# Attention on one Trainium2 core: normalization and output of four blocks inside the group loop, in place of 14 batches at the end

## The chip, the cores and the metric

The kernel runs on one core of a Trainium2 chip. A core has TensorE (PE), VectorE (DVE), ScalarE (ACT), GpSimd (POOL) and SyncE (SP, which here only issues DMAs). They run beside one another and are ordered by semaphores. The metric is device time in microseconds (us), the median of several executions.

## The reference

A graph of 12500 nodes with 128 numbers each and 212500 edges, sorted by destination. A first layer (relation-wise products, a sum over the edges, a feed-forward part) gives `x`; the second layer is attention over each node's incoming edges:

```python
h = relu(layernorm(x))
xt = (h @ W.T + bias).reshape(n, 4, 32)
alpha = leaky_relu(alpha_src[row] + alpha_dst[col], 0.2)
ex = exp(alpha - segment_max(alpha, col)[col])
denom = segment_sum(ex, col)
alpha = ex / (denom[col] + 1e-16)
x = x + segment_sum(xt[row] * alpha[..., None], col).reshape(n, 128)
```

The kernel divides at the end: it sums `ex * xt[row]` and `ex` per node and head, and the last step is `x + sum / (denom + 1e-16)`.

## The kernel before

The nodes are 98 blocks of 128 rows (`BLOCKS`); a block lies across the 128 partitions. The edges are 104 groups of 2048 (16 chunks of 128, `CHUNKS`), sorted by destination, so a group touches one or two neighbouring blocks. `MAIN` = 103 groups go through the main loops; the last one and any that touch more blocks go through a loop over a list.

The span has three stages. To about 260 us the products of all blocks are stored as a table. To about 2440 us POOL gathers rows of that table for every group (L486, 16 indirect DMAs for a group), PE sums them per node, and after every four groups the dense part of four blocks (a quad) is computed and stored (`x_mid`, `xt_table`). The first `AHEAD` = 24 quads run in that loop; what is left, the last quad and those that touch a listed group, is in the list `redo` with its length `redo_count`, last quad first. `first_of(n)` is the first block of quad n: 0, then 4n - 2.

From about 2450 us on the attention stage runs, over 103 groups in order. POOL gathers the group's rows of `xt_table` into one of four slots of `G`, 16 indirect DMAs each; it waits for the indices and for the messages of the group four before. DVE has one round for a group: `nodes` (L1164 to L1177: maxima and state of the block), `scores` of the next group (L1152, which waits for that group's gather), `edges` (L1187 to L1194), `merge` of the group before (L1215, L1218: it adds PE's sums into `S`, which holds for each node and head 32 sums and the denominator), the selection matrix (L1198), the messages (L1204), and `prepare` for the group after next (L1135 to L1142). PE forms maxima, slots and sums from these, ACT the exponentials. The loop (L1290) has 25 iterations of four rounds; groups 101 and 102 follow written out, then the last merge (L1306).

Each DVE operation whose result the next one needs is followed by a wait on a counting semaphore (`Chain.step`). Where an index is a register, it is computed or loaded on the engine's own sequencer (`load_block`, `load_redo_count`).

The end is at L1308 to L1318: for each of 14 batches of seven blocks DVE adds 1e-16 to the denominators, takes the reciprocal, multiplies, and adds `x_res`, the layer's input, which four DMAs (L431) brought back at about 2448 us. SP stores a batch as soon as `fin_done` says so (L434 to L440). `A`, `Y` and `X` are tiles of one quad that the dense part uses and the attention stage does not.

Of the kernel before, what the change touches and what calls it, by code (L numbers as in the profile page):

```python
# [13 lines left out]
P = 128  # L14
N, E, D, R, H = 12500, 212500, 128, 8, 512
HEADS, HC = 4, 32
BLOCKS = -(-N // P)
TAIL_ROWS = N - (BLOCKS - 1) * P
CHUNKS = 16
GROUP = CHUNKS * P  # L20
GROUPS = -(-E // GROUP)
BATCH = 7
BATCHES = BLOCKS // BATCH
SPARE = BATCH
WIDE = 14
ROUNDS = BLOCKS // WIDE
TURNS = 3
FIRST_TURN = 2
XT = D + HEADS
HD = HC + 1  # L30
RUNS = 4
MAIN = GROUPS - 1
SLOTS = 4
QUAD = 4
SHIFT = 2
QUADS = -(-(BLOCKS + SHIFT) // QUAD)
LAG = 2
AHEAD = GROUPS // SLOTS - LAG
# [8 lines left out]
assert (BLOCKS + SHIFT) % QUAD == 0 and BLOCKS % WIDE == 0 and FIRST_TURN + -(-2 * CHUNKS // TURNS) <= WIDE and BLOCKS % BATCH == 0 and GROUPS % SLOTS == 0 and BLOCKS % 2 == 0 and (MAIN - 3) % SLOTS == 0  # L47
# [8 lines left out]
def first_of(n):  # L56

    return max(n * QUAD - SHIFT, 0) if isinstance(n, int) else n * QUAD - SHIFT
# [87 lines left out]
def build(nc, x, src, dst, typ, W_rel, W_self, b_conv, g1, b1n, g2, b2n, W1, b1, W2, b2,  # L146
# [7 lines left out]
    with ctx:  # L154
# [52 lines left out]
        redo = sb("redo", [1, QUADS], i32)  # L207
# [25 lines left out]
        place = sb("place", [P, 3])  # L233
        rel0 = sb("rel0", [P, CHUNKS])
# [53 lines left out]
        out_sb = g_flat[:, 0:4 * BATCH * D].rearrange("p (s b d) -> p s b d", s=4, d=D)  # L288
        inv = g_flat[:, 4 * BATCH * D:4 * BATCH * D + 4 * BATCH * HEADS].rearrange("p (s b h) -> p s b h", s=4, h=HEADS)

# [71 lines left out]

        def load_redo_count(eng):

            return eng.value_load(redo_count[0:1, 0:1], min_val=1, max_val=QUADS)
# [13 lines left out]
        def _(sp):  # L379
# [54 lines left out]
            for q in range(BATCHES):  # L434
                sp.wait_ge(fin_done, q + 1)
                lo = q * BATCH
                nb = BATCH - 1 if q == BATCHES - 1 else BATCH
                sp.dma_start(out[lo * P:(lo + nb) * P, :].rearrange("(b p) d -> p b d", p=P), x_res[:, lo:lo + nb, :]).then_inc(s_out, 16)
            sp.dma_start(out[(BLOCKS - 1) * P:N, :], x_res[0:TAIL_ROWS, BLOCKS - 1, :]).then_inc(s_out, 16)
            sp.wait_ge(s_out, 16 * (BATCHES + 1))  # L440
# [298 lines left out]
        def _(dve):  # L739
# [195 lines left out]
            c.beside(v.tensor_copy(redo[:, :], banks[2][0:1, 256:256 + QUADS]))  # L935
# [342 lines left out]
            def round_of(c, gr, s, k, first, last, landed):  # L1278

                nodes(groups, c, gr, gr, first)  # L1280
                if landed:
                    scores(groups, c, (s + 1) % SLOTS, 1 - k, landed)
                edges(groups, c, gr, s, k, (lambda: merge(groups, c, gr - 1, gr - 1, last, 1 - k)) if last is not None else (lambda: None))
# [6 lines left out]
            with dve.Fori(0, (MAIN - 3) // SLOTS) as i:  # L1290
                last = load_block(dve, i * SLOTS)
                for s in range(SLOTS):
                    gr = i * SLOTS + s + 1
                    c = Chain(dve, c_att, gr * PASS + START - MISSED)
                    first = load_block(dve, gr)
                    round_of(c, gr, (s + 1) % SLOTS, (s + 1) % 2, first, last,
                             (gathered[1][(s + 2) % SLOTS], i * (16 * CHUNKS) + 16 * CHUNKS * (1 + (s + 2) // SLOTS)))
                    prepare(groups, c, row_of(nkey_all, gr + 2), row_of(run_all, gr + 2), (s + 1) % 2)
                    assert c.n == PASS
                    last = first  # L1300
            for gr in (MAIN - 2, MAIN - 1):
                c = Chain(dve, c_att, gr * PASS + START - MISSED - (STEPS["prep"] if gr == MAIN - 1 else 0))
                last, first = load_block(dve, gr - 1), load_block(dve, gr)
                round_of(c, gr, gr % SLOTS, gr % 2, first, last,
                         (gathered[1][(gr + 1) % SLOTS], 16 * CHUNKS * ((gr + 1) // SLOTS + 1)) if gr + 1 < MAIN else None)
            merge(groups, c, MAIN - 1, MAIN - 1, first, (MAIN - 1) % 2)  # L1306

            dve.wait_ge(s_back, 16 * -(-BLOCKS // (2 * WIDE)))  # L1308
            c = Chain(dve, c_fin)
            for q in range(BATCHES):  # L1310
                s = q % 4
                lo = q * BATCH
                f = S[:, lo:lo + BATCH, :].rearrange("p b (h k) -> p b h k", h=HEADS)
                c.step(v.tensor_scalar(inv[:, s, :, :], f[:, :, :, HC:HD].rearrange("p b h o -> p b (h o)"), 1e-16, None, ALU.add))
                c.step(v.reciprocal(inv[:, s, :, :], inv[:, s, :, :]))
                c.step(v.tensor_tensor(out_sb[:, s, :, :].rearrange("p b (h k) -> p b h k", h=HEADS), f[:, :, :, 0:HC],  # L1316
                                       inv[:, s, :, :].rearrange("p b (h o) -> p b h o", o=1).to_broadcast([P, BATCH, HEADS, HC]), ALU.mult))
                v.tensor_tensor(x_res[:, lo:lo + BATCH, :], x_res[:, lo:lo + BATCH, :], out_sb[:, s, :, :], ALU.add).then_inc(fin_done, 1)  # L1318
# [246 lines left out]
```

## Time and profile before

| | us |
|---|---|
| median of 3 runs | 4616.43 (4613.22 to 4616.86) |
| the profiled execution | 4617.47 |
| its span | 4615.6 |

| engine | busy us | share of the span |
|---|---|---|
| PE (matmul) | 2439.7 | 53% |
| DVE | 2518.3 | 55% |
| ACT | 537.3 | 12% |
| POOL | 3200.9 | 69% |

The span is what the profiler records from the first to the last instruction; it stands beside the execution's own time. A share is an average over stages that have different limits, so the stage has to be looked at in which the change works. POOL's instructions here are the gathers; an idle time put down to "issue" is one in which the engine waited for nothing that the profile shows.

### The profile page before, as it was taken

To read this page: it belongs to the slowest core of one execution; us is meant where nothing else is said; L and a number is where in the kernel's file an instruction comes from. 1 tells how busy PE (TensorE), PEld (TensorE's weight loads), DVE (VectorE), ACT (ScalarE), POOL (GpSimd) and SP (SyncE) were. 2 spreads that over 40 slices of the span, in tenths; PEclk is the share of its full clock that TensorE was granted. 3 is DMA by queue.
4 is the path that set the end of the run, shared out by engine and by line. 5 is a ranking of instruction groups with operands and counts; after the bars stand their busy time and mean duration, and the time that the engine had idled before them with its cause. 6 is when DMAs were issued, how large, how long until landed. Compare 5 with 4: busy or idle time off the path is not lost.

```text
span 4615.6 us, 52499 instructions
## 1 busy us (share of the span) xinstructions
PE 2439.7 (53%) x13699; PEld 2082.5 (45%) x13804; DVE 2518.3 (55%) x6796; ACT 537.3 (12%) x1405; POOL 3200.9 (69%) x3372
## 2 busy tenths in 40 slices
PE   5952344343444444343433666666666666666664
PEld 2532333333333333333323555555555555555553
DVE  5761333333333333333333777777777777777777
ACT  2410111111111111111111000000000000000000
POOL 1057777777777777777755777777777777777772
PEclk9976666676666666666666777777787777777776
DMA  6632222222222222222213222222222222222222
GB/s 205 254 108 53 57 57 62 57 62 57 59 59 58 61 57 62 57 62 57 59 42 98 55 54 55 55 55 54 55 54 54 54 54 55 54 55 54 55 55 76
DMA packets 169505, 312.22 MB, mean 68 GB/s; under 512 B 58788, under 2 KB 99148, under 8 KB 168655
## 3 DMA queue, kind: packets, MB, share of 16 engines
q0 software_dynamic: 107008, 222.77, 20.1%
q1 hardware_dynamic: 49586, 82.57, 4.9%
q10 hardware_dynamic: 12754, 5.49, 0.5%
q14 instruction: 145, 1.19, 0.1%
q8 instruction: 12, 0.20, 0.0%
HBM read 239.51 MB, written 71.09 MB: 67 GB/s over the span
## 4 chain that ended last, share of the span: by engine, by line
POOL 67%; issue 23%; PE 5%; DVE 2%; DMA 1%; ACT 0%; POOLq 0%; ACTq 0%; DVEq 0%; SPq 0%
POOL G L486 67%; PE bank L1342 1%; PE bank L1343 1%; PE quad L1342 1%; PE quad L1343 1%; DMA rel_table<-G 1%; DMA x_res<-in_x 0%; DVE G L1316 0%; DVE x_res L1318 0%; PE bank L1385 0%; ACT agg L697 0%; PE quad L1414 0%; PE bank L1344 0%; PE quad L1344 0%; PE quad L1420 0%
## 5 line engine op out<-in xcount | busy, mean ns | idle before, releaser
L486 POOL DMA_INDIRECT G<-rel_table,idx x1680 | 1603.3, 954 | 778.4 <-issue 511.4
L486 POOL DMA_INDIRECT G<-xt_table,idx x1664 | 1576.8, 948 | 543.1 <-issue 506.8
L962 DVE SCALAR_TENSOR_TENSOR agg<-bank,sel,agg 128x128 f32 x208 | 63.6, 347 | 1139.6 <-PE bank L1385 1138.1
L1484 PEld LDWEIGHTS quad<-ident,top 128*128 128x128 f32 x3328 | 557.2, 262 | 103.0 <-issue 98.5
L1484 PE MATMUL quad<-ident,top 128*128 128x128 f32 x3328 | 557.7, 346 | 43.8 <-DVEq L1155 43.8
L1512 PE MATMUL bank<-M,onehot 128*128 128x132 f32 x3328 | 457.9, 295 | 172.4 <-DVE M L1204 172.4
L1512 PEld LDWEIGHTS bank<-M,onehot 128*128 128x128 f32 x3328 | 423.7, 204 | 204.2 <-issue 204.2
L1385 PE MATMUL bank<-G,onehot 128*128 128x128 f32 x1664 | 265.1, 334 | 389.1 <-DMA G<-rel_table,idx 384.8
L1385 PEld LDWEIGHTS bank<-G,onehot 128*128 128x128 f32 x1664 | 261.1, 251 | 393.8 <-issue 393.8
L1500 PE MATMUL bank<-Z,w_all 128*128 128x8 f32 x832 | 170.7, 334 | 498.7 <-issue 492.7
L1385 PE MATMUL bank<-G,M 128*128 128x128 f32 x1664 | 264.6, 334 | 274.1 <-DMA G<-rel_table,idx 264.2
L1500 PEld LDWEIGHTS bank<-Z,w_all 128*128 128x128 f32 x832 | 164.0, 293 | 515.8 <-issue 515.8
L1385 PEld LDWEIGHTS bank<-G,M 128*128 128x128 f32 x1664 | 258.1, 249 | 278.9 <-issue 278.9
L1409 PE MATMUL quad<-ident,A 128*128 128x128 f32 x200 | 54.3, 426 | 564.0 <-ACT A L627 564.0
L1409 PEld LDWEIGHTS quad<-ident,A 128*128 128x128 f32 x200 | 35.7, 217 | 572.1 <-issue 572.1
L1204 DVE TENSOR_TENSOR M<-G,bank 128x256 f32<-128x256 f32 (+2 forms) x312 | 251.2, 860 | 18.5 <-DVE onehot L1198 18.5
L1168 DVE TENSOR_REDUCE tops<-quad 128x4 f32<-128x2048 f32 x104 | 238.3, 2291 | 29.1 <-DVE Z L1165 19.7
L1198 DVE TENSOR_TENSOR onehot<-iota,bank 128x2048 f32<-128x2048 f32 x104 | 237.8, 2287 | 3.8
L1479 PE MATMUL quad<-ident,w_all 128*128 128x512 bf16 x312 | 148.3, 610 | 68.7 <-DVEq L1144 46.5
L1414 PE MATMUL quad<-Y,w 128*128 128x512 f32 x200 | 146.6, 851 | 16.9 <-ACT Y L644 16.9
L706 ACT ACTIVATE fade<-fade_arg 128x8 f32<-128x8 f32 x104 | 21.7, 209 | 1145.6 <-DVEq L1179 1145.6
L1420 PEld LDWEIGHTS quad<-w,w_all 128*128 128x128 f32 x800 | 121.0, 220 | 53.0 <-issue 33.4
(312 smaller groups left out, 3231.9 us busy)
## 6 DMA issues: line engine op xcount, KB each, us to landing
rel_table<-G SPq DMA_DIRECT2D x98, 512.0 KB, 2.6
G<-rel_table,idx POOLq DMA_INDIRECT x1680, 2.5
G<-xt_table,idx POOLq DMA_INDIRECT x1664, 2.7
xt_table<-w_all SPq DMA_DIRECT2D x25, 264.0 KB, 3.2
x_mid<-X SPq DMA_DIRECT2D x25, 256.0 KB, 2.0
out<-x_res SPq DMA_DIRECT2D x13, 448.0 KB
x_res<-x_mid SPq DMA_DIRECT2D x3, 1792.0 KB, 10.9
x_res<-in_x ACTq DMA_DIRECT2D x9, 448.0 KB, 22.6
```

What stands on the lines that cost most here:

```text
L486: g.indirect_dma_start(out=G[:, s, c, 0:width], out_offset=None, in_=table, in_offset=bass.IndirectOffsetOnAxis(ap=idx[:, s, c:c + 1], axi ...
L1168: c.step(v.tensor_reduce(tops[:, :], quad[:, :].rearrange("p (j h e) -> p h j e", j=RUNS, h=HEADS), AX.XY, ALU.max))
L1198: v.tensor_tensor(onehot[:, :, :], iota1[:, :].rearrange("p (o e) -> p o e", o=1).to_broadcast([P, CHUNKS, P]), pick_key[:, k, :].rearrang ...
L1204: v.tensor_tensor(M[:, lo:hi, :, 0:HC], G[:, s, lo:hi, 0:D].rearrange("p c (h k) -> p c h k", h=HEADS), banks[7][:, lo * HEADS:hi * HEADS] ...
L1342: t.matmul(banks[2 + 3 * s][:, :], hT[:, s, :], w_all[:, 512:1024], start=True, stop=True).then_inc(xwB_ps, 1)
L1385: ins = t.matmul(banks[5 + k][:, 0:D], picks[k][:, c, :], G[:, s, c, 0:D], start=(c == 0), stop=(c == CHUNKS - 1))
L1414: t.matmul(banks[1 + c % 2][:, :], w1[:, c * P:(c + 1) * P], tT, start=True, stop=True).then_inc(up_ps, 1)
L1420: ins = t.matmul(banks[3][:, j * D:(j + 1) * D], hid[:, c % 2, j * P:(j + 1) * P], w2[:, c, :], start=(c == 0 and j == 0), stop=(c == H // ...
L1479: t.matmul(banks[j][:, :], miss[:, k, j, :], ident4[:, :, :].rearrange("p h e -> p (h e)"), start=True, stop=False)
L1484: ins = t.matmul(banks[j][:, hd * P:(hd + 1) * P], top[:, j, hd:hd + 1].to_broadcast([P, P]), ident[:, :], start=False, stop=(hd == HEADS ...
L1500: ins = t.matmul(banks[5][:, j * 2 * HEADS:(j + 1) * 2 * HEADS], hit[:, j, :], Z[:, 1:3, :].rearrange("p a h -> p (a h)"), start=True, sto ...
L1512: ins = t.matmul(banks[6][:, 0:XT], onehot[:, c, :], M[:, c, :, :].rearrange("p h k -> p (h k)"), start=(c == 0), stop=(c == CHUNKS - 1))
```

## The change

The batches and their stores go. A function `finish` does the same four operations for one quad, into a tile of its own (`A` in the loop, `Y` for late quads, `X` for the last), and DVE calls it in the second round of an iteration, between `nodes` and `scores`, for the quad that became complete (`LAG` = 2 iterations behind). The loop over iterations is therefore split: two iterations without it, one written out with quad 0, and a loop over the other 22. Quad 23 is finished in the round of group 102. After the last merge a loop over the number of entries in `redo` finishes late quads, from the second entry on; `redo` has one entry more, which is zero. Then the last quad is finished into `X`. SP stores each quad when it is finished; a tile is written again only when its last store has landed.

```diff
-        redo = sb("redo", [1, QUADS], i32)
+        redo = sb("redo", [1, QUADS + 1], i32)
...
+        inv = sb("inv", [P, QUAD, HEADS])
...
-        out_sb = g_flat[:, 0:4 * BATCH * D].rearrange("p (s b d) -> p s b d", s=4, d=D)
-        inv = g_flat[:, 4 * BATCH * D:4 * BATCH * D + 4 * BATCH * HEADS].rearrange("p (s b h) -> p s b h", s=4, h=HEADS)
...
+        def load_late(eng, i):
+
+            return eng.value_load(redo[0:1, bass.ds(i, 1)], min_val=0, max_val=first_of(AHEAD) - QUAD)
...
-            for q in range(BATCHES):
-                sp.wait_ge(fin_done, q + 1)
-                lo = q * BATCH
-                nb = BATCH - 1 if q == BATCHES - 1 else BATCH
-                sp.dma_start(out[lo * P:(lo + nb) * P, :].rearrange("(b p) d -> p b d", p=P), x_res[:, lo:lo + nb, :]).then_inc(s_out, 16)
-            sp.dma_start(out[(BLOCKS - 1) * P:N, :], x_res[0:TAIL_ROWS, BLOCKS - 1, :]).then_inc(s_out, 16)
-            sp.wait_ge(s_out, 16 * (BATCHES + 1))
+            def store_out(n, lo, tile):
+
+                sp.wait_ge(fin_done, n + 1)
+                sp.dma_start(out[bass.ds(lo * P, QUAD * P), :].rearrange("(b p) d -> p b d", p=P), tile[:, :, :]).then_inc(s_out, 16)
+
+            store_out(0, first_of(0), A)
+            with sp.Fori(1, AHEAD) as n:
+                store_out(n, first_of(n), A)
+            n = load_redo_count(sp)
+            with sp.Fori(0, n) as i:
+                store_out(i + AHEAD, load_late(sp, i + 1), Y)
+            sp.wait_ge(fin_done, n + (AHEAD + 1))
+            tail = BLOCKS - 1 - first_of(AHEAD)
+            sp.dma_start(out[first_of(AHEAD) * P:(BLOCKS - 1) * P, :].rearrange("(b p) d -> p b d", p=P), X[:, 0:tail, :]).then_inc(s_out, 16)
+            sp.dma_start(out[(BLOCKS - 1) * P:N, :], X[0:TAIL_ROWS, tail, :]).then_inc(s_out, 16)
+            sp.wait_ge(s_out, n * 16 + 16 * (AHEAD + 2))
...
-            c.beside(v.tensor_copy(redo[:, :], banks[2][0:1, 256:256 + QUADS]))
+            c.beside(v.memset(redo[:, QUADS:], 0))
+            c.beside(v.tensor_copy(redo[:, 0:QUADS], banks[2][0:1, 256:256 + QUADS]))
...
-            def round_of(c, gr, s, k, first, last, landed):
+            def finish(n, lo, tile, stored):
+
+                f = S[:, bass.ds(lo, QUAD), :].rearrange("p b (h k) -> p b h k", h=HEADS)
+                c = Chain(dve, c_fin, n * 3)
+                if stored is not None:
+                    dve.wait_ge(s_out, stored)
+                dve_stop(dve)
+                c.step(v.tensor_scalar(inv[:, :, :], f[:, :, :, HC:HD].rearrange("p b h o -> p b (h o)"), 1e-16, None, ALU.add))
+                c.step(v.reciprocal(inv[:, :, :], inv[:, :, :]))
+                c.step(v.tensor_tensor(tile[:, :, :].rearrange("p b (h k) -> p b h k", h=HEADS), f[:, :, :, 0:HC],
+                                       inv[:, :, :].rearrange("p b (h o) -> p b h o", o=1).to_broadcast([P, QUAD, HEADS, HC]), ALU.mult))
+                v.tensor_tensor(tile[:, :, :], tile[:, :, :], x_res[:, bass.ds(lo, QUAD), :], ALU.add).then_inc(fin_done, 1)
+
+            def round_of(c, gr, s, k, first, last, landed, done=None):
 
                 nodes(groups, c, gr, gr, first)
+                if done is not None:
+                    finish(done, first_of(done), A, done * 16 if not isinstance(done, int) or done else None)
                 if landed:
                     scores(groups, c, (s + 1) % SLOTS, 1 - k, landed)
...
-            with dve.Fori(0, (MAIN - 3) // SLOTS) as i:
+            def four_rounds(i, done):
+
...
+            with dve.Fori(0, LAG) as i:
+                four_rounds(i, None)
+            dve.wait_ge(s_back, 16 * -(-BLOCKS // (2 * WIDE)))
+            four_rounds(LAG, 0)
+            with dve.Fori(LAG + 1, (MAIN - 3) // SLOTS) as i:
+                four_rounds(i, i - LAG)
...
+                         AHEAD - 1 if gr == MAIN - 1 else None)
             merge(groups, c, MAIN - 1, MAIN - 1, first, (MAIN - 1) % 2)
 
-            dve.wait_ge(s_back, 16 * -(-BLOCKS // (2 * WIDE)))
-            c = Chain(dve, c_fin)
-            for q in range(BATCHES):
...
+            n = load_redo_count(dve)
+            with dve.Fori(0, n) as i:
+                finish(i + AHEAD, load_late(dve, i + 1), Y, i * 16 + 16 * AHEAD)
+            finish(n + AHEAD, first_of(AHEAD), X, None)
```

## Rows read from the trace of the kernel before

**Rows 1.** The page's chain that ended last, by engine

```profile
POOL 67%; issue 23%; PE 5%; DVE 2%; DMA 1%; ACT 0%; POOLq 0%; ACTq 0%; DVEq 0%; SPq 0%
```

**Rows 2.** Busy time by stretch: us, each engine's busy (instructions), clock, DMA share, GB/s

```profile
2520.00:4500.00 1980.00, 1279.68 (x7839) 1144.82 (x7937) 1480.19 (x3463) 129.48 (x496) 1498.27 (x1581) 0.78 0.24 55
```

**Rows 3.** POOL's groups, 420 to 2340, then 2520 to 4500: busy, mean ns | idle before

```profile
L486 POOL DMA_INDIRECT G<-rel_table,idx x1533 | 1453.8, 948 | 467.2 <-issue 467.2
...
L486 POOL DMA_INDIRECT G<-xt_table,idx x1581 | 1498.4, 948 | 481.8 <-issue 481.8
```

**Rows 4.** Waits from 2600 to 4500 us: us in total, times, longest

```profile
DVE w L1152 <- DMA G<-xt_table,idx: 81.6, 50, 2.1
```

**Rows 5.** DVE in order of time, one iteration: start, duration, operation [idle before]

```profile
3401.95 0.61 DVE L1152 TENSOR_TENSOR w<-G,w 128x256 f32<-128x256 f32 x1 [2.02 <-DMA G<-xt_table,idx]
...
3418.58 0.34 DVE L1164 TENSOR_SCALAR Z<-am,sel 128x8 f32 x1 [4.59 <-issue]
...
3437.12 0.23 DVE L1164 TENSOR_SCALAR Z<-am,sel 128x8 f32 x1 [0.98 <-DVE w_all L1142]
...
3442.26 0.61 DVE L1152 TENSOR_TENSOR w<-G,w 128x256 f32<-128x256 f32 x1 [0.26 <-DVE fade_arg L1177]
...
3462.24 0.61 DVE L1152 TENSOR_TENSOR w<-G,w 128x256 f32<-128x256 f32 x1 [1.72 <-DMA G<-xt_table,idx]
```

**Rows 6.** All engines in order of time, from the loop's end to the last merge

```profile
4537.74 0.23 DVE L1164 TENSOR_SCALAR Z<-am,sel 128x8 f32 x1 [1.68 <-issue]
...
4541.29 0.94 POOL L486 DMA_INDIRECT G<-xt_table,idx  x1 [0.30 <-issue]
...
4543.92 0.61 DVE L1152 TENSOR_TENSOR w<-G,w 128x256 f32<-128x256 f32 x1 [1.36 <-DMA G<-xt_table,idx]
...
4551.95 2.42 DVE L1204 TENSOR_TENSOR M<-G,bank 128x256 f32<-128x256 f32 x3 [0.18 <-DVE onehot L1198]
...
4558.66 0.36 DVE L1177 TENSOR_SCALAR fade_arg<-diff,sel 128x4 f32<-128x4 f32 x2
...
4559.38 1.01 DVE L1187 TENSOR_TENSOR w<-w,bank 128x512 f32<-128x512 f32 x1 [0.36 <-PE bank L1500]
...
4573.02 0.43 DVE L1215 TENSOR_TENSOR agg<-agg,fade 128x264 f32 x1 [4.54 <-issue]
4573.49 0.62 DVE L1218 SCALAR_TENSOR_TENSOR agg<-bank,sel,agg 128x132 f32 x2
```

**Rows 7.** In order of time, the first batch and the last operation

```profile
4574.14 0.18 DVE L1314 TENSOR_SCALAR G<-agg 128x28 f32<-128x28 f32 x1
4574.36 0.33 DVE L1315 RECIPROCAL G<-G 128x28 f32<-128x28 f32 x1
4574.72 1.09 DVE L1316 TENSOR_TENSOR G<-agg,G 128x896 f32<-128x896 f32 x1
...
4611.05 1.09 DVE L1318 TENSOR_TENSOR x_res<-x_res,G 128x896 f32<-128x896 f32 x1
```

**Rows 8.** Waits of SP's DMA queue, whole span: us in total, times, longest

```profile
SPq L438 <- DVE x_res L1318: 2157.5, 14, 2127.4
```

**Rows 9.** The page's DMA issues: count, KB each, median us to landing

```profile
x_mid<-X SPq DMA_DIRECT2D x25, 256.0 KB, 2.0
```

**Rows 10.** In order of time, DVE and POOL in the last quad's dense part

```profile
2412.06 0.69 DVE L1019 TENSOR_TENSOR Y<-Y,A 128x512 f32<-128x512 f32 x1 [0.89 <-ACT A L640]
2412.68 0.94 POOL L486 DMA_INDIRECT G<-rel_table,idx  x1 [0.30 <-issue]
2412.87 0.69 DVE L1020 TENSOR_TENSOR X<-x_res,Y 128x512 f32<-128x512 f32 x1
```

**Rows 11.** In order of time, DVE behind register loads and at a loop's end

```profile
2386.97 0.06 DVE L1086 MEMSET place<- 128x3 f32 x1 [3.36 <-issue]
...
2389.06 0.17 DVE L1098 TENSOR_TENSOR dist<-rel 128x16 f32<-128x16 f32 x1 [0.80 <-DVE low L1095]
...
2400.66 1.89 DVE L1113 SCALAR_TENSOR_TENSOR nkey_all<-run_all,nkey_all 128x1664 bf16<-128x1664 bf16 x1 [0.55 <-DVE place L1108]
```

More of the change, by code:

```diff
@@ L46 @@
 HEAD, MIDDLE = 4, 8
-assert (BLOCKS + SHIFT) % QUAD == 0 and BLOCKS % WIDE == 0 and FIRST_TURN + -(-2 * CHUNKS // TURNS) <= WIDE and BLOCKS % BATCH == 0 and GROUPS % SLOTS == 0 and BLOCKS % 2 == 0 and (MAIN - 3) % SLOTS == 0
+assert AHEAD - 1 == (MAIN - 3) // SLOTS - LAG and (BLOCKS + SHIFT) % QUAD == 0 and BLOCKS % WIDE == 0 and FIRST_TURN + -(-2 * CHUNKS // TURNS) <= WIDE and BLOCKS % BATCH == 0 and GROUPS % SLOTS == 0 and BLOCKS % 2 == 0 and (MAIN - 3) % SLOTS == 0
 f32, bf16 = mybir.dt.float32, mybir.dt.bfloat16
@@ L431, in _ @@
                 sp.dma_start(x_res[:, lo:hi, :], x_mid[:, lo:hi, :]).then_inc(s_back, 16)
-            for q in range(BATCHES):
-                sp.wait_ge(fin_done, q + 1)
-                lo = q * BATCH
-                nb = BATCH - 1 if q == BATCHES - 1 else BATCH
-                sp.dma_start(out[lo * P:(lo + nb) * P, :].rearrange("(b p) d -> p b d", p=P), x_res[:, lo:lo + nb, :]).then_inc(s_out, 16)
-            sp.dma_start(out[(BLOCKS - 1) * P:N, :], x_res[0:TAIL_ROWS, BLOCKS - 1, :]).then_inc(s_out, 16)
-            sp.wait_ge(s_out, 16 * (BATCHES + 1))
+            def store_out(n, lo, tile):
[12 more added lines that the diff above has]
+            sp.wait_ge(s_out, n * 16 + 16 * (AHEAD + 2))
+            sp_stop(sp)
         @block.gpsimd
@@ L1296, in _ @@
                     round_of(c, gr, (s + 1) % SLOTS, (s + 1) % 2, first, last,
-                             (gathered[1][(s + 2) % SLOTS], i * (16 * CHUNKS) + 16 * CHUNKS * (1 + (s + 2) // SLOTS)))
+                             (gathered[1][(s + 2) % SLOTS], i * (16 * CHUNKS) + 16 * CHUNKS * (1 + (s + 2) // SLOTS)), done if s == 1 else None)
                     prepare(groups, c, row_of(nkey_all, gr + 2), row_of(run_all, gr + 2), (s + 1) % 2)
@@ L1304, in _ @@
                 round_of(c, gr, gr % SLOTS, gr % 2, first, last,
-                         (gathered[1][(gr + 1) % SLOTS], 16 * CHUNKS * ((gr + 1) // SLOTS + 1)) if gr + 1 < MAIN else None)
+                         (gathered[1][(gr + 1) % SLOTS], 16 * CHUNKS * ((gr + 1) // SLOTS + 1)) if gr + 1 < MAIN else None,
+                         AHEAD - 1 if gr == MAIN - 1 else None)
             merge(groups, c, MAIN - 1, MAIN - 1, first, (MAIN - 1) % 2)
-            dve.wait_ge(s_back, 16 * -(-BLOCKS // (2 * WIDE)))
-            c = Chain(dve, c_fin)
-            for q in range(BATCHES):
[L1311 to L1318, printed above, removed]
+            n = load_redo_count(dve)
+            with dve.Fori(0, n) as i:
+                finish(i + AHEAD, load_late(dve, i + 1), Y, i * 16 + 16 * AHEAD)
+            finish(n + AHEAD, first_of(AHEAD), X, None)
         @block.tensor
```

## The prediction

> **What bounds the kernel now.** I read the profile in this order: the chain that ended last, the stages, the loop of the attention stage, and its last 75 us.
>
> The chain gives 67% of the span to POOL's gathers, 23% to issue gaps and 2% to DVE [rows 1]. In the attention stage proper, 2520 to 4500 us, POOL waits for nothing but its own issue gap: 1581 gathers of 948 ns and 0.30 us before each, (1498.4 + 481.8) us, fill the 1980 us [rows 3]. A group of 16 gathers takes 20.05 us, an iteration of four groups 80.2 us. DVE is busy 1480 of those 1980 us [rows 2], but it is not the bound: it waits for gathers to land, 81.6 us in all over 24 iterations, 3.4 us an iteration [rows 4]. [rows 5] show the pattern: a stall of 4.59 us at the top of the loop (before L1164), then no wait for a gather in the scores of the second round (0.26 us before L1152, which is what the semaphores cost there; the first round is the same), 1.72 us in the third, and 2.02 us in the fourth, just before the next top.
>
> After the last gather nothing hides DVE. POOL's last descriptor work ends at 4542.23, DVE starts on its data at 4543.92, and from then on DVE is the chain, with one wait for PE's sums (4.54 us) [rows 6]. The last merge ends at 4573.49 + 0.62 = 4574.11. Then come the 14 batches, 2.71 us each, to 4611.05 + 1.09 = 4612.14 [rows 7], and 3.46 us for the last two stores up to the span's end at 4615.6. So 38.03 us of DVE work stand bare, while DVE had waited for gathers in the loop.
>
> **The change part by part.**
>
> *How many quads.* The dense stage stored 25 quads [rows 9]. 24 (AHEAD) of them run in its main loop, so the list of late quads has one entry, the one at block 94: n = 1. In the new kernel quads 0 to 22 are finished in the loop (iterations 2 to 24), quad 23 in the round of group 102, then comes one pass of the tail loop (for n = 1 it redoes block 0, since the list's second entry is the new zero), and the last quad from X. Three quads of bare work instead of 14 batches of seven blocks.
>
> *One quad's price.* An addition of 16 numbers per partition, 0.17 us (0.18 for 28); a reciprocal of 16, between 0.17 and the 0.33 of 28 [rows 7], I take 0.25; two 128x512 operations at 0.69, the measured time of that form on SBUF tiles (L1020) [rows 10] (4/7 of the batch's 1.09 would be 0.62, the lower bound); three gaps of 0.04. Sum 1.9 us. Where block numbers come from registers, 0.1 more for three operations: the gap before L1020 is 0.12 instead of 0.04 [rows 10]. So 2.2 us.
>
> *Removed:* 14 batches, 38.03 us.
>
> *In the loop, 23 times.* The quad's four operations, register arithmetic for its block, and a wait on the store of the quad before, which was issued 80 us earlier and is long landed (an equal store lands in 2.0 us [rows 9]). Queued behind it on DVE are scores, edges, merge and prepare; PE's maxima wait for the scores, ACT's exponentials and PE's sums for the edges. I put it at 2.3 us net; below 1.9 (nothing for registers), above 3.4 (its first operation as late as L1164 behind a register load, 0.98 us [rows 5]). The slack is 3.4 us less the 0.26 that stays in each of two rounds, 2.9 us an iteration. The finish stands in the second round; rounds three and four give back 1.5 and 1.8 us, so DVE is on the gathers' pace again before the next loop top. POOL does not notice: its next gather goes to the slot whose messages were made some 28 us before (L1204 ends at 4554.4, 12 us after the next group's gather; two rounds earlier that is 12 - 40 = -28) [rows 6]. Price of the loop: 0. If the cover were gone, it would be 2.3 x 23 = 53 us.
>
> *Stores.* SP waited in all 2157.5 us for batches, once for 2127.4, with an empty queue [rows 8]; 24 stores of 256 KB now lie in that stretch, ahead of nothing that anybody waits for. In the dense stage 25 such stores ran beside the same gathers [rows 9], whose mean is 948 ns there as here [rows 3]. Price 0, at most 24 x 0.1 us.
>
> *DVE beside the gathers.* Do four more operations hold POOL up? The gather beside L1019 and L1020, two-input fp32 operations of exactly the added form, takes 0.94 us [rows 10]. All that POOL loses above 0.94 in the whole stage is 1498.4 - 1581 x 0.94 = 12 us, with 1480 us of DVE work beside it [rows 2, 3]; 43 us more would take 0.3 us. The Trainium skill (SBUF — State Buffer, "SBUF: two separate sides") speaks against the change here: while DVE runs an operation in a two-port mode, GpSimd cannot write descriptors and its DMAs starve. The same page ("Who interferes with whom") excepts tensor_tensor, and the trace agrees with that exception, at 0.94 us.
>
> *Round of group 102.* Here nothing covers. The quad starts 0.3 us after L1177 (ended 4559.02) and takes 1.9, static; the 0.36 us wait for PE before L1187 [rows 6] disappears in it. Price 1.85 us (1.5 to 2.6).
>
> *After the last merge.* A register load of the count, entry of the loop, a second register load for the block, the wait. One such load is worth 0.80 us (before L1098), four with a loop's entry 3.36 us (before L1086) [rows 11]; two at the end of the main loop took 1.68 us, at 4537.74 [rows 6]. I take 2.0; bounds 1.2 and 3.4. Then a quad with registers 2.2, the loop's end 0.5 (0.55 before L1113 [rows 11], 0.1 below), the last quad 1.9.
>
> *Last stores.* As before two follow the last operation, 192 and 42 KB where it was 384 and 42; 2.0 of the 3.46 us are the landing even of a 256 KB store [rows 9]. I take 3.4, down to 2.9.
>
> *Plan stage and straight code.* One memset of a number beside others: at most 0.1 us. Iteration 2 written out removes two loop tops from DVE, which is not the bound there: 0.
>
> *Sum.* 4574.11 + 1.85 + 2.0 + 2.2 + 0.5 + 1.9 = 4582.56, + 3.4 = 4586.0. Against 4615.6 that is 29.6 us less. The profiled execution took 4617.47, so 4587.9; the median of the runs shown is 1.0 lower (4616.43): **4586.8 us**, 0.64% less.
>
> **The rivals.**
>
> *The slack is too small (8%).* If a finish in the loop costs more than 2.9 us, DVE falls behind by the rest every iteration; POOL, with 28 us in hand, is still not held, and all of it shows at the end. At the bound of 3.4 us: 0.5 x 21 = 10 us, 4597 us. For it: the 4.59 us at the loop's top show that this sequencer has costs of its own; against: no register load is in the added code.
>
> *The tail pays a stall of its own (7%).* If entering or leaving the tail's loop costs what the main loop's top costs (4.59 us instead of 0.98) [rows 5], 3.6 us are added once or twice: 4590.4 to 4594. Against: the code lies in a straight line and the loop is left, not repeated. The Trainium skill (Runtime: NRT & Kernel Launch, "Instruction fetch mechanics") says that a taken branch out of the fetched window stalls and that straight code does not; the trace agrees so far, with 4.59 us at a repeated top and 1.68 us where the loop is left.
>
> *It is slower: the new operations hold POOL (3%).* If POOL's descriptor work stood still for the whole of each added quad, every one of the 23 would put its 1.9 us on the chain, since POOL is the bound: 44 us lost against 29.6 won, 4631 us. It decides from 29.6/23 = 1.3 us per finish. Against: the gather of 0.94 us beside L1019 and L1020 [rows 10]. The SBUF page's rule without its exception would give this.
>
> *It does not do what it says (2%).* If more late quads were on the list than the 25 stores show, each would add 2.2 us, and with one tile Y for all a store's landing of 2.0 and its issue of 0.4: three of them, 14 us, 4601 us.
>
> **How the numbers follow.** The forecast has 80%. Its own range: down 0.8 for the tail's loads, 0.4 for the loop's end, 0.3 for the quads, 0.5 for the stores, 0.3 for group 102, and 1.5 by which runs differ, 4583; up 1.4 for the loads, 0.8 for group 102, 2.4 for stores beside gathers and 1.5, 4593. The range of 8 in 10, taken with the unknown costs, reaches on to the first rival: 4583 to 4597. A measurement of this kernel can tell 0.2%, 9.2 us. Faster by more: the forecast, the second rival, and most of the first and the last, 0.94; within: 0.03; slower: 0.03.
>
> **What would show each step.** In the new profile: POOL with nothing but its 0.30 us gaps, 948 ns a gather, the last one ending at 4542 still; DVE's wait for gathers down from 3.4 to about 1 us an iteration, not gone; 24 groups of four finish operations between 2680 and 4562 us and two more behind the last merge; SP with a store every 80 us. It is wrong if DVE no longer waits for any gather in the late iterations (lag), if POOL's mean rises over 0.95 us, if more than two quads follow the last merge, or if more than 3.4 us lie between the last merge and the tail's first operation.

## The result and the profile after

The changed kernel takes 4600.12 us, the median of seven runs (4586.87 to 4605.44), against 4614.7 for the kernel before (4612.81 to 4616.86, seven runs): a ratio of 0.9964 [0.9951, 0.9977], 0.36% faster. The forecast was 4586.8, 0.64% less, in a range of 4583 to 4597. The sign came out as forecast, the size did not: about half of the gain is missing, and the median lies 3 us above the range.

The profiled execution is the fastest of the seven, 4586.87 us with a span of 4585.1. The forecast for the span was 4586.0. That looks like a hit and is none, which only a comparison stage by stage shows. First the chain that ended last, by engine, of the changed kernel:

```profile
POOL 40%; DVE 28%; issue 22%; PE 5%; DVEq 3%; DMA 1%; ACT 1%; POOLq 0%; ACTq 0%; SPq 0%
```

Before, POOL had 67% and DVE 2% [rows 1]; now DVE has 28%. DVE has become the bound of the attention stage. Then the stretch of the attention stage (us, each engine's busy time with instructions, clock, DMA share, GB/s):

```profile
2520.00:4500.00 1980.00, 1256.49 (x7731) 1125.93 (x7830) 1508.66 (x3517) 127.56 (x490) 1498.17 (x1582) 0.78 0.25 58
```

and from the page POOL's group for its gathers:

```profile
L498 POOL DMA_INDIRECT G<-xt_table,idx x1664 | 1576.2, 947 | 543.0 <-issue 501.0
```

POOL is as it was [rows 2, 3]: 947 ns a gather, 1582 of them in the stretch. DVE is busy 28 us more, not a shift that should turn the bound. The waits of DVE from 2600 to 4500 us (us in total, times, longest) tell more:

```profile
DVE Z L1177 <- issue: 138.4, 23, 7.0
...
DVE w L1165 <- DMA G<-xt_table,idx: 12.8, 8, 2.2
```

DVE waited for gathers 81.6 us before [rows 4]; now it is 12.8 us, eight times in all, the last before 2820 us; from there on it waits for none, where it went on waiting to the end before. It is late. And the stall at the loop's top, on which nothing works, is 6 us and more in each iteration, 138.4 in all. One iteration, in order of time:

```profile
3406.12 0.23 DVE L1177 TENSOR_SCALAR Z<-am,sel 128x8 f32 x1 [6.49 <-issue]
...
3429.34 0.36 DVE L1190 TENSOR_SCALAR fade_arg<-diff,sel 128x4 f32<-128x4 f32 x2
3430.19 0.17 DVE L1298 TENSOR_SCALAR inv<-agg 128x16 f32 x1 [0.49 <-DVE fade_arg L1190]
...
3431.64 0.69 DVE L1302 TENSOR_TENSOR A<-A,x_res 128x512 f32<-128x512 f32 x1 [0.16 <-DVE A L1300]
3432.25 0.60 DVE L1165 TENSOR_TENSOR w<-G,w 128x256 f32<-128x256 f32 x1
```

The finish costs 3432.25 - 3429.70 = 2.55 us from the end of L1190 to the scores, less the 0.26 that lay there before: 2.29 us, where 2.3 was forecast. What grew, unforeseen, is the stall at the loop's top, 6.4 to 6.5 us where it was 4.59 [rows 5]. The tops of 20 iterations later give the period:

```profile
2837.79 0.23 DVE L1177 TENSOR_SCALAR Z<-am,sel 128x8 f32 x1 [6.33 <-issue]
...
4462.61 0.23 DVE L1177 TENSOR_SCALAR Z<-am,sel 128x8 f32 x1 [6.39 <-issue]
```

(4462.61 - 2837.79)/20 = 81.24 us an iteration, while POOL makes four groups in 80.2. DVE loses 1.04 us each time, 21 us over 20 iterations. The end of the stage shows it whole:

```profile
4520.26 0.94 POOL L498 DMA_INDIRECT G<-xt_table,idx  x1 [0.30 <-issue]
...
4544.14 0.61 DVE L1165 TENSOR_TENSOR w<-G,w 128x256 f32<-128x256 f32 x1 [0.26 <-DVE fade_arg L1190]
...
4576.12 0.62 DVE L1231 SCALAR_TENSOR_TENSOR agg<-bank,sel,agg 128x132 f32 x2
4578.57 0.17 DVE L1298 TENSOR_SCALAR inv<-agg 128x16 f32 x1 [1.83 <-issue]
...
4581.83 0.69 DVE L1302 TENSOR_TENSOR X<-X,x_res 128x512 f32<-128x512 f32 x1
```

The last gather's descriptors end at 4521.20, the scores of that group start 22.94 us later; before it was 1.69 [rows 6]. So DVE is 21.25 us behind. But POOL ended 21.03 us earlier than in the profiled execution of before, and that has nothing to do with the change: its first gather of the stage already starts earlier by as much.

```profile
2438.16 0.94 POOL L498 DMA_INDIRECT G<-xt_table,idx  x1 [36.16 <-ACT idx L733]
```

In the kernel before that line stands at 2458.67:

```profile
2458.67 0.94 POOL L486 DMA_INDIRECT G<-xt_table,idx  x1 [36.31 <-ACT idx L721]
```

The ledger of the span against the forecast: POOL's early start -21.0, lag +21.25, the round of group 102 +0.6, everything behind the last merge -1.6; -0.8 in all, and with more digits the 0.9 between 4586.0 and 4585.1. Two differences of 21 us, neither of them forecast, cancel by luck. Two questions follow: what makes the stall at the top grow, and why do executions start 20 us apart?

### The profile page after: what moved, and what is told of

It reads as the page before. It is cut to its first block, busy times and chain, and to the rows that moved or that the text cites. A ratio compares the mean times of both kernels' runs of the same rounds, so it can differ in the third digit from the quotient of the medians.

```text
span 4585.1 us, 52779 instructions
## 1 busy us (share of the span) xinstructions
PE 2433.3 (53%) x13699; PEld 2078.9 (45%) x13804; DVE 2522.2 (55%) x6845; ACT 537.1 (12%) x1405; POOL 3199.1 (70%) x3372
## 4 chain that ended last, share of the span: by engine, by line
POOL 40%; DVE 28%; issue 22%; PE 5%; DVEq 3%; DMA 1%; ACT 1%; POOLq 0%; ACTq 0%; SPq 0%
POOL G L498 40%; DVE onehot L1211 4%; DVE tops L1181 4%; DVE M L1217 3%; DVE w L1200 2%; DVE edge L1203 1%; DVEq L341 1%; DVE w_all L1155 1%; DVE w L1165 1%; DVE agg L1231 1%; DVE top L1167 1%; PE bank L1372 1%; PE bank L1373 1%; DVE agg L1228 1%; PE quad L1372 1%
## 5 line engine op out<-in xcount | busy, mean ns | idle before, releaser
L1514 PEld LDWEIGHTS quad<-ident,top 128*128 128x128 f32 x3328 | 540.4, 254 | 102.7 <-issue 97.3
L1542 PE MATMUL bank<-M,onehot 128*128 128x132 f32 x3328 | 470.0, 300 | 191.9 <-DVE M L1217 191.9
L1514 PE MATMUL quad<-ident,top 128*128 128x128 f32 x3328 | 538.3, 338 | 47.2 <-DVEq L1168 47.2
L1542 PEld LDWEIGHTS bank<-M,onehot 128*128 128x128 f32 x3328 | 435.9, 209 | 223.5 <-issue 223.5
L1177 DVE TENSOR_SCALAR Z<-am,sel 128x8 f32 x104 | 24.7, 237 | 220.9 <-issue 146.7
```

The lines of the kernel that those rows point to most:

```text
L1514: ins = t.matmul(banks[j][:, hd * P:(hd + 1) * P], top[:, j, hd:hd + 1].to_broadcast([P, P]), ident[:, :], start=False, stop=(hd == HEADS ...
L1542: ins = t.matmul(banks[6][:, 0:XT], onehot[:, c, :], M[:, c, :, :].rearrange("p h k -> p (h k)"), start=(c == 0), stop=(c == CHUNKS - 1))
```

## The experiments

**Theories.** For the lag, theory A: DVE's need per iteration exceeds the period (finish 2.3 + 1.8 more of stall, against 2.9 of slack), and the growth of the stall comes from where the longer loop lies in DVE's instruction stream (theory P in the expectations). Rival B: DVE seems late only in an execution in which POOL started early, and would not be late otherwise. Rival C (rival L in the expectations): the stall belongs to the longer body, with the finish's registers and waits in it, and would stay wherever the code lay. For the start, theory S: it depends on when `x` lands beside the edge lists' loads, and not on the change.

The queue of instruction fetches bears on theory A. Its line in a view of the DMAs (packets, MB, share of 16 engines) from 3000 to 4440 us, which is some 18 iterations, before:

```profile
q14 instruction: 90, 0.74, 0.2%
```

and after:

```profile
q14 instruction: 88, 0.72, 0.2%
```

These are packets of some 8 KB, five for each iteration in both kernels: part of the loop is fetched again each time round. Within the stall alone, 3399.6 to 3406.1 us, the changed kernel's trace has three, some 2.5 us apart, in the quarters of a microsecond from 3400.75, 3403.25 and 3405.75 on; within that of before, 3414.0 to 3418.5, it has two (from 3415.0 and 3417.5 on).

```profile
q14 instruction: 3, 0.02, 1.3%
```

```profile
q14 instruction: 2, 0.02, 1.3%
```

The third starts behind 3405.9, less than 0.2 us before the stall's end, and in the loop moved by 128 below even behind it (stall to 3342.51, third fetch between 3342.51 and 3342.75). So the number of fetches goes with the size of the stall, but the landing of the third isn't what DVE waited for.

The Trainium skill (Runtime: NRT & Kernel Launch, "Instruction fetch mechanics") says that a taken branch out of the fetched window waits for a DMA of its target. The trace agrees with the kind: the wait stands at the branch back and nowhere else in the body. By the same page the window is two blocks of 16 KiB, against which stand the 8 KB of the packets here (packets of 16 KB there are on another instruction queue, q8: 12 with 0.20 MB before).

**The changed kernel once more** (no edit; a_again).

> The changed kernel once more, for a second profile and more times. Two things differed in its first profile from what was forecast, and cancelled: DVE fell behind the gathers in the attention loop (the scores of group 102 started at 4544.1 while POOL's last gather had ended at about 4521.8, 20 us of lag), and the first loads of x landed at 10.0 us instead of 23.0 us, with everything to the attention stage 20 us earlier. Theory A (lag and an early start are independent; the start varies from execution to execution): executions between 4587 (early start) and 4606 (start as before), none much lower or higher; in every profile the same stall of about 6.4 us at the top of the second attention loop and the same lag of about 20 us, whatever the start. Rival B (the early start causes the lag, since the gathers come early): in a profile with a late start the lag is near 0 and the stall 4.6 us, and the time is still about 4586.

Measured: 4606.02 us (4587.37 to 4608.65, 11 runs) beside 4612.6 for the kernel before on the same chip, 0.9978 [0.9964, 0.9993]. This profiled execution started late, its span is 4604.3. The end of the stage:

```profile
4542.06 0.94 POOL L498 DMA_INDIRECT G<-xt_table,idx  x1 [0.30 <-issue]
...
4564.68 0.61 DVE L1165 TENSOR_TENSOR w<-G,w 128x256 f32<-128x256 f32 x1 [0.26 <-DVE fade_arg L1190]
```

POOL ends where it did before the change, and DVE is 4564.68 - 4543.00 - 1.69 = 20.0 us behind all the same. Rival B falls: the lag is there with a late start too. The runs lie in two bands: three of the 11 at 4587 to 4591, eight at 4603 to 4609. The kernel before has them too, 6 of 21 runs at 4598 to 4601, the rest at 4610 to 4618. Band against band the change is worth 8 to 11 us (medians 4590.1 against 4600.7, and 4607.3 against 4615.5), which is the forecast of 29.6 less the lag of 21.

**The loop moved by 36 instructions** (a_pad36). It removes nothing and adds no work to the loop; 36 tiny memsets stand ahead of the attention stage.

```diff
+        pad = sb("pad", [1, 200])
...
+            for k in range(36):
+                v.memset(pad[:, k:k + 1], 0.0)
             dve.wait_ge(tables_ready[1], 1)
```

> 36 tiny memsets of a spare tile stand on DVE ahead of the attention stage, where DVE waits 20 us for a gather anyway; they do nothing but move all later DVE instructions by 36 places. The top of the second loop was at instruction 22 of a block of 256 by my count and is now at 58, where the old kernel's loop top was. Theory P (the stall at a repeated loop top depends on where top and end lie in the instruction stream, and the move of the loop made it 6.4 us instead of 4.6): the stall falls to 4.6 us, an iteration of DVE falls from 81.2 to below 80.2, so DVE waits for gathers again, the lag goes and the time is 4586 to 4588 with a start as before, about 4567 with an early one. Rival L (the longer body makes the stall, wherever it lies): the stall stays 6.4 us and the time as the changed kernel's, 4587 to 4606.

Measured: 4577.97 us (4565.81 to 4586.04, four runs), 0.9921 [0.9894, 0.9947]. The stall and the end of the stage, in order of time:

```profile
3415.40 0.30 DVE L1178 TENSOR_SCALAR Z<-am,sel 128x8 f32 x1 [2.13 <-issue]
...
4539.99 0.94 POOL L499 DMA_INDIRECT G<-xt_table,idx  x1 [0.30 <-issue]
...
4542.66 0.61 DVE L1166 TENSOR_TENSOR w<-G,w 128x256 f32<-128x256 f32 x1 [1.00 <-DMA G<-xt_table,idx]
```

DVE's waits from 2600 to 4500 us:

```profile
DVE w L1166 <- DMA G<-xt_table,idx: 100.4, 70, 2.3
...
DVE Z L1178 <- issue: 52.9, 24, 4.6
```

The same loop, with the same finish in it, stalls 2.13 us instead of 6.4. From 3000 to 4440 us there is no line of the instruction queue left, and over the whole span it has 34 packets instead of 139:

```profile
q14 instruction: 34, 0.28, 0.0%
```

DVE waits for gathers again, 100.4 us, and is on POOL's pace at the end. From POOL's end to the span's end it takes 4583.3 - 4540.93 = 42.4 us, where it was 4615.6 - 4542.23 = 73.4: 31.0 us less, against 29.6 forecast. Rival C falls: the stall depends on where the loop lies, and the same body with the finish in it stalls less. I had expected it to return to 4.6; a loop that stays resident, at 2.1, was not foreseen.

**Moved by 128** (a_pad128; the same diff with `range(128)`).

> The same with 128 memsets: the loop top at place 150 of 256, its end at 195 of the next block. Theory P: the stall differs from that of the changed kernel (6.4 us) and from that with 36; by how much I can't say. Rival L: 6.4 us again, and the first of the two loops, 290 instructions long by my count against 301, keeps 4.8 us in all three.

Measured: 4609.05 us (4594.28 to 4612.93, ten runs), 0.9989 [0.9974, 1.0004].

```profile
3342.51 0.23 DVE L1178 TENSOR_SCALAR Z<-am,sel 128x8 f32 x1 [6.68 <-issue]
```

and the instruction queue from 3000 to 4440 us:

```profile
q14 instruction: 89, 0.73, 0.2%
```

The stall is that of the unmoved loop, and so are the fetches. I had expected it to differ. By hindsight it would fit blocks of 128 instructions, one to a packet, of which a shift by a whole block changes nothing; no run measured how many instructions a packet holds. Of the expectation's rival L one part came true: the first loop, two iterations long, keeps its one stall (4.78 us unmoved, 4.65 moved by 36, 4.74 by 128). It has 2.17 us when moved by 200, so its stall too depends on the place. The 128 memsets themselves delay the stage's first gather by 4 us: it comes 40.2 us after the gather before it, where it was 36.2.

**The loop unrolled twice** (a_unroll2).

```diff
-            with dve.Fori(LAG + 1, (MAIN - 3) // SLOTS) as i:
-                four_rounds(i, i - LAG)
+            with dve.Fori(0, ((MAIN - 3) // SLOTS - LAG - 1) // 2) as h:
+                for k in range(2):
+                    four_rounds(h * 2 + (LAG + 1 + k), h * 2 + (1 + k))
```

> The changed kernel with two iterations written out in the body of the second attention loop (11 iterations of eight rounds instead of 22 of four). Half of the loop tops go: per eight rounds DVE needs one stall less, 5 to 6 us, that is 81.2 - 2.8 = 78.4 us per four rounds, below the gathers' 80.2. If the lag is what costs (theory A with either P or L): DVE waits for gathers again, the last group's scores start with its gather, and the time is 4586 to 4588 with a start as before, about 4567 with an early one. Rival (DVE's added operations themselves are too long, not the stalls): DVE needs 2.3 us of 3.2 for them, so this would leave the lag at 10 us or more.

Measured: 4577.2 us (4567.41 to 4585.55, four runs), 0.9933 [0.9909, 0.9957]. The starts of two sets of four rounds, one behind the other:

```profile
3316.54 0.23 DVE L1177 TENSOR_SCALAR Z<-am,sel 128x8 f32 x1 [1.72 <-issue]
...
3400.32 0.28 DVE L1177 TENSOR_SCALAR Z<-am,sel 128x8 f32 x1 [6.36 <-issue]
```

and DVE's waits from 2600 to 4500 us:

```profile
DVE Z L1177 <- issue: 87.1, 23, 6.6
...
DVE w L1165 <- DMA G<-xt_table,idx: 50.2, 31, 2.2
```

Where the code runs straight on there are 1.72 us, behind the branch 6.36: 4.6 us less per eight rounds, 2.3 an iteration, more than the 1.04 that was lacking. The lag is gone, and the span (early start) is 4565.7 against 4585.1: -19.4.

**A chip on which all is slower.** Four kernels ran on a chip where the kernel before takes 6239.64 us, 35% longer: the changed kernel with `x` loaded first (a_xfirst), that one unrolled too (u_xfirst), the kernel before moved by 64 memsets (b_pad64), and the changed kernel moved by 200 (a_pad200). Their edits stand below, where they ran again.

> The changed kernel, and SP loads the edge lists only when the first two batches of x have landed. Seen so far: executions of both kernels fall into two bands some 15 to 20 us apart (the old one 4598 to 4601 and 4610 to 4618, the changed one 4587 to 4591 and 4603 to 4609), and the profiles with an early first gather (251.9 and 252.8 us) are those in which DVE's first statistics start at 10 to 11 us and not at 17 to 23. Theory S (the band is set in the first 40 us, by when x lands beside the edge lists and whether DVE's first norm chain then meets POOL's work on the edges, and has nothing to do with the change): with x first, the statistics start at or below 11 us in every execution, the first gather at about 252 us, and all executions lie in the low band, 4585 to 4591 us; stall and lag in the attention stage stay as they are, 6.4 us and 20 us. Rival (the bands come from elsewhere, the instruction fetch or the chip): two bands again.

> x first as in the run before, and the second attention loop with two iterations in its body. If both causes are what they seem, they add: no high band and no lag, 4565 to 4570 us in all executions, against the old kernel's 4598 to 4618. Rival: with everything 20 us earlier and no lag something else comes late, and a part of the gain goes.

> The old kernel with 64 tiny memsets of a spare tile on DVE ahead of the attention stage, where it waits; they only move its later instructions. Theory P: the stall at the loop top changes with the position (4.6 us before; 2.1 us, 4.6 or 6.5 now, by whether the loop still has instructions fetched in each iteration), and the time does not, since DVE waits for gathers there: same as before within 0.2% in the same band; the waits for gathers take up the difference (3.4 us an iteration before, 5.9 if the stall is 2.1, 1.5 if it is 6.5). Rival (the position does nothing in a loop of 290 instructions): 4.6 us as before.

> The changed kernel moved by 200 places. So far: moved by 0 and by 128 places 6.4 to 6.5 us of stall and about five fetches of 8 KB of instructions an iteration; moved by 36 places 2.1 us and no fetch at all. 8 KB are 128 instructions of 64 bytes, so 128 places are a whole block and change nothing, which fits; 200 places are 72 beyond a block. Theory B (the loop's 301 instructions lie in three or in four blocks of 128, by where the top falls in a block, and only with three are all still there when the loop jumps back): the stall is either 2.1 us with no fetch, or above 4.5 us with fetches, nothing between; 72 is most likely still good (2.1 us), as the window of good positions is up to 84 places wide and 36 is in it. Rival: the stall takes a third value and the fetches are not all or nothing.

Measured, in that order: 6091.53 us (four runs), ratio 0.9761 [0.9741, 0.9782]; 6081.54 (five), 0.9752 [0.9736, 0.9767]; 6232.19 (ten), 0.9989 [0.9975, 1.0002]; and one run at 6077.61, without an interval. A wait of POOL in the first of them, 3200 to 6000 us:

```profile
POOL G L499 <- DVE M L1218: 919.9, 66, 22.2
```

Here POOL waits for DVE's messages, in the changed kernel as in the moved one of before (962.1 us there); the gathers are no longer the bound, and the times that were expected rest on a balance that doesn't hold here. The stalls can be compared all the same. Two tops of the loop in a_xfirst, and one in b_pad64:

```profile
3819.20 0.23 DVE L1178 TENSOR_SCALAR Z<-am,sel 128x8 f32 x1 [6.39 <-issue]
...
4175.10 0.23 DVE L1178 TENSOR_SCALAR Z<-am,sel 128x8 f32 x1 [17.46 <-issue]
```

```profile
4326.06 0.23 DVE L1165 TENSOR_SCALAR Z<-am,sel 128x8 f32 x1 [16.83 <-issue]
```

Most tops of a_xfirst stall 6.2 to 6.6 us, and most of a_pad200 4.6 to 5.0: the place gives the size that it gives on the other chips. Beside that come longer waits, up to 17.5 us, at some tops and in other rounds (9.12 us before the round at 3896.97). They are not fetches of DVE's instructions: b_pad64 has 16.83 us at a top, 485.5 us of such waits before L1165 from 3200 to 6000 us, and in all that time no packet on q14, where a_xfirst has 116. What makes them stayed open.

All three forms of the changed kernel take 2.4 to 2.6% less there, but two of them also load `x` first. Of the 145 us between the spans of b_pad64 and a_xfirst, 29 lie ahead of the attention stage, 64 in its gathers and 52 behind the last one. Why an iteration is some 3 us shorter (119.1 us against 122.0), though it has more work, was not settled.

**`x` loaded first** (a_xfirst2). Theory S says that the two bands come from the loads at the start. The kernel before, first 40 us, DVE's first operation on `x` and one of those behind it, and POOL's work on the edge lists:

```profile
23.08 2.62 DVE L745 BATCH_NORM_STATS2 stats<-x_res 128x6 f32<-128x128 f32 x13 [22.95 <-DMA x_res<-in_x]
...
31.02 4.50 POOL L464 TENSOR_TENSOR M<-M,G 104x2048 f32<-104x2048 f32 x1
31.21 4.35 DVE L752 TENSOR_SCALAR wide_rstd<-wide_rstd 128x14 int32<-128x14 int32 x1
```

The profiled execution of the changed kernel, same place:

```profile
10.08 2.61 DVE L757 BATCH_NORM_STATS2 stats<-x_res 128x6 f32<-128x128 f32 x13 [9.96 <-DMA x_res<-in_x]
...
14.75 0.17 DVE L764 TENSOR_SCALAR wide_rstd<-wide_rstd 128x14 int32<-128x14 int32 x1
```

`x` landed at 23 us in one and at 10 in the other, and that later chain then met POOL's work: an operation on 14 numbers took 4.35 us instead of 0.17. The chain's last operation (L764 before, L776 after) ends at 41.59 in one and 17.72 in the other, 23.9 us apart, of which 13.0 are the landing and 10.9 operations that took longer. The edit lets SP wait for `x` before it issues the loads of the edge lists:

```diff
+            sp.wait_ge(s_x[0], 16 * (WIDE // BATCH))
```

> Again, since the chip of the first attempt took 35% longer for every kernel, the old one included (6240 us), and had stalls of up to 34 us everywhere, so that the bands of 15 to 20 us could not be seen there. On a chip on which the old kernel takes 4600 to 4618: theory S as before, statistics at or below 11 us, the first gather at 252 us, all executions in the low band of the changed kernel, 4585 to 4591 us, with the 6.4 us stall and the lag of 20 us unchanged. Rival: two bands.

Measured: 4586.52 us (4584.84 to 4590.4, four runs), 0.994 [0.9924, 0.9957]; the kernel before had 4615.29 there, none of its 13 runs under 4613.

```profile
9.10 2.61 DVE L758 BATCH_NORM_STATS2 stats<-x_res 128x6 f32<-128x128 f32 x13 [8.98 <-DMA x_res<-in_x]
```

All four runs lie in the early band, and the stall (6.36 us) and a lag of some 19.5 us are still there. The bands come from the start, the lag doesn't. Without this edit 14 of 38 runs of the changed kernel, moved or unrolled ones with it, were early, with it eight of eight, these and the four of the next run.

**Both mends together** (u_xfirst2: `x` first and the loop unrolled).

> x first, and two iterations in the body of the second attention loop. 4565 to 4570 us in all executions if the two causes add; if something else comes late, more than 4572.

Measured: 4566.41 us (4564.3 to 4570.09), 0.9894 [0.9878, 0.9911]. It beats both kernels: 48.9 us less than before.

```profile
4522.87 0.94 POOL L499 DMA_INDIRECT G<-xt_table,idx  x1 [0.30 <-issue]
...
4525.53 0.61 DVE L1166 TENSOR_TENSOR w<-G,w 128x256 f32<-128x256 f32 x1 [1.39 <-DMA G<-xt_table,idx]
```

POOL ends early, and DVE waits for the last gather again.

**The kernel before, moved by 64** (b_pad64_2: 64 memsets ahead of its attention stage).

> The old kernel, DVE's later instructions moved by 64 places. Theory P: another stall than 4.6 us at the loop top (2.1 us without any fetch in the loop, or up to 6.5 us), no other time beyond the two bands of the old kernel, 4598 to 4601 and 4610 to 4618, and DVE's wait for gathers takes up the difference. Rival: 4.6 us as before.

Measured: 4612.08 us (4596.29 to 4615.25, ten runs), 0.9989 [0.9979, 0.9998]. Its waits from 2600 to 4500 us:

```profile
DVE w L1153 <- DMA G<-xt_table,idx: 154.9, 96, 2.1
...
DVE Z L1165 <- issue: 50.2, 24, 2.1
```

The stall of the old loop also falls to 2.1 us, with no fetch in the loop, and the time stays within 0.2%: what DVE saves it waits for gathers (154.9 us instead of 81.6). The slack of the kernel before depended on the place of its loop, 2.9 us an iteration as profiled and 5.4 so (154.9/24 = 6.5, less 0.26 in each of four rounds), and nothing in its time showed that.

**The changed kernel moved by 200** (a_pad200_2: `range(200)`, 72 more than a block of 128).

> The changed kernel moved by 200 places, 72 beyond a block of 128. Theory B: a stall of 2.1 us with no instruction fetched in the loop, or one above 4.5 us with fetches, nothing between; 2.1 is the likelier. With 2.1 us the time is 4566 to 4571 or 4583 to 4588 by band, with 6.4 us 4587 to 4591 or 4603 to 4609.

Measured: 4577.29 us (two runs, both with an early start), 0.9917 [0.9898, 0.9937].

```profile
3329.28 0.23 DVE L1178 TENSOR_SCALAR Z<-am,sel 128x8 f32 x1 [4.75 <-issue]
```

and DVE's waits from 2600 to 4500 us:

```profile
DVE Z L1178 <- issue: 105.1, 24, 5.0
...
DVE w L1166 <- DMA G<-xt_table,idx: 26.5, 30, 2.0
```

I had held 2.1 for likelier; it became 4.75, with two fetches in the stall, as in the kernel before. Even that is enough: need and period are about equal (26.5 us of waits for gathers are left), and there is no lag. That the time is 7 to 11 us above the other early runs without a lag comes from the memsets: 200 of them put the stage's first gather 44.0 us after the gather before it, where it was 36.2. The stall comes in three sizes then, 2.1, 4.6 to 4.75 and 6.4 to 6.7 us, and the last two go with two and three fetches. Which place gives which I could not derive: a rule of whole blocks that fits the shifts by 0, 36 and 128 gives a resident loop for 200 too.

## Why the prediction was wrong, and where it was right

*What bounds the kernel.* Right: POOL's gathers bounded the stage, DVE had a small slack, and nothing covers what follows the last gather.

*The price of the loop: 0.* This is the step that failed. Its first half was right: the finish costs 2.29 us (forecast 2.3). The second half compared it with a slack of 2.9 us that I read from the waits for gathers and held for fixed. In that slack stood a stall of 4.59 us at the loop's top, which I had seen and named, and which I took as a constant; the change makes the loop longer and moves it, and the stall rose by 1.8 to 6.4. Need 80.2 - 2.9 + 2.3 + 1.8 = 81.4 us against 80.2. The lag of 21 us is the 1.04 us of each iteration, added up; the loop moved by 36 instructions shows that the stall is its cause. It is the first rival in kind (slack too small, POOL not held, all of it at the end), which I gave 8% and 10 us. Its trigger, a finish dearer than 2.9, did not occur. "No register load is in the added code", the argument against it, was true and beside the point: the loop's length and place were what counted.

*POOL not held.* Right. Its mean stayed 947 ns, and its last gather has only the usual 0.30 us before it even with DVE 21 us late, inside the 28 us that the forecast gave it. The rival of the held POOL fell; the Trainium skill's exception for tensor_tensor (SBUF — State Buffer, "Who interferes with whom") agrees with these rows.

*Stores in the loop: 0.* Right: 24 stores of 256 KB, and the gathers as before.

*Round of group 102.* The quad took 1.73 us of the path (forecast 1.85). Unforeseen are 0.6 us more of waiting for PE's sums, 5.13 where it was 4.54 [rows 6].

*After the last merge.* 1.83 us to the tail's first operation (2.0), one late quad 2.04 (2.2), the loop's end nothing to be seen (0.5), the last quad 1.9 (1.9), and 2.6 us for the last stores (3.4): 8.36 in all against 10.0. The rival of a stall in the tail fell. That n = 1, and with it 24 quads ahead of the last merge, one `Y` and one `X`, was right. (By the code, the zero that this pass reads is the second of the list's 25 entries and was there before; the added one is the 26th.)

*The sum.* With the stall out of the way the change takes 31.0 us from the stretch behind POOL's last gather, with 29.6 forecast. So the sum for the end came within 1.4 us, its parts somewhat too dear, and the one for the loop was short of a term of 21 us.

*The range.* It took three runs of before, all within 4 us, as the spread. Over 21 runs of the same kernel there are two bands, with medians 15 us apart, from the start alone. With the lag the changed kernel's medians were 4600.12 and 4606.02; which of the bands a set of seven runs shows is chance, and the range held neither that nor the lag.

*The signs to look for.* "It is wrong if DVE no longer waits for any gather in the late iterations (lag)" named the view in which the error showed. The profiled time by itself would have confirmed the forecast to 1 us.

## What to carry to other kernels

Where an engine has only a few microseconds of slack in a long loop, a stall at the loop's top is no constant: any edit that makes the loop longer or moves it can change it, here by 2.5 us from the smallest size to the next and by 1.8 more to the largest, so look for the instruction queue inside the loop and price the edit with the stall at each size seen. Small overdrafts add up over the iterations while the bounding engine still looks untouched, and unrolling the loop took them away here, as did moving it by 36 or 200 instructions, but not by 128. And compare two executions stage by stage from the first line on, since a time that matches the forecast can be two errors that cancel.

## What the runs showed of the hardware

The wait behind a branch back took three sizes for the same body: 2.1 us with no fetch, 4.6 to 4.75 with two, 6.4 to 6.7 with three, the fetches some 2.5 us apart. Of the 2.1 us some 1.7 are no matter of the branch: where the code runs straight on and also loads two block numbers, the gap is 1.68 us [rows 6] and 1.72 (a_unroll2). On the slower chip most tops of the changed kernel had the same sizes, and longer waits, up to 17.5 us, came beside them, with fetches and without.

At the start DVE was held by POOL, the other way round from what one usually looks for: an operation of DVE on 14 numbers, 0.17 us alone, took 4.35 us and ended at 35.56, where POOL's operation on 2048 numbers ended at 35.52. The Trainium skill (SBUF — State Buffer, "Who interferes with whom") says that the engine which issues second can be blocked for the whole of the other's instruction; the trace agrees. With the late landing of `x` it makes 23.9 us at the chain's end, of which 18 are left at the first gather (269.67 and 251.86 us); how much each of the two would cost alone was not tested.

Open remain the rule by which a place gives a size of the stall, what DVE waits for in the largest one once the second fetch has landed, the waits of up to 17.5 us on the slower chip, and the larger gain there.
